# Two-byte count matrices, spread edge keys, early residual tiles, and seven block products in the last expert layer of a graph transformer kernel

## The chip, the cores and the metric

The kernel runs on one core of a Trainium2 chip. The metric is the device time of one execution in microseconds (us). Five engines work side by side and meet only at semaphores: PE (TensorE, matmuls and transposes), DVE (VectorE), ACT (ScalarE), POOL (GpSimd) and SP (SyncE), which here only issues transfers. All arithmetic on PE is fp32; the trace records each fp32 matmul as two MATMUL rows, so a row count is twice the number of matmuls in the code.

## What is computed

Two layers over a graph of 1250 nodes with 768 features. Each layer runs a linear-attention mixer, a two-step graph attention (GAT) and a mixture of experts, each with a residual. What matters here is cut from the reference:

```python
# edges: 10000 random pairs both ways + 1250 self loops (21250), sorted by dst
# layer 0 mixer: phi = exp(q @ rf.T - |q|^2/2); out = attn @ proj_w.T + proj_b
# layer 0 and 1 GAT, per head:
e     = leaky_relu(as_[src] + ad_[dst], 0.2)
m     = segment_max(e, dst);  w = exp(e - m[dst]);  z = segment_sum(w, dst)
out   = segment_sum(h[src] * (w / z[dst])[:, None], dst)
# layer 1 experts: 8 experts of width 128, top 2 of 8 per node
y     = sum_e gate[n, e] * (silu(x @ w1[e].T) @ w2[e].T)
```

The kernel doesn't walk edges in the GATs. It makes a dense 1250 x 1250 matrix that holds how often each (source, target) pair occurs, multiplies dense attention weights by it, and uses a second form of it (minus a large number where the count is zero) for the maxima.

## The kernel before

**Sizes.** Nodes are ten tiles of T = 125 rows (NT = 10). PSUM is split in two rings: five banks "V" drained by DVE and three banks "A" drained by ACT. `plan()` writes out by hand the order in which all banks are filled and drained; `V_AT` and `A_AT` give each its number, and `fill` on PE and `bank` on DVE and ACT follow it. A fill waits until the bank five (or three) fills back has been drained. All three engines run their queues strictly in order.

**Keys (the count of duplicates).** The 21250 edges lie as 125 x 170 (EC = 170 columns). `KEY` = source x 1250 + target. For each column, PE transposes the keys into a row (L550, four columns make one of 43 key groups) and DVE compares all pairs of that column (L1366), so that duplicates within one column are summed before they are scattered. After each fifth group DVE prepares 20 columns of indices (L1379 to L1383, `index_made`). `KEYS_BESIDE` and `KEYS_BESIDE_QK` say after which fill how many key groups stand: before, two behind each of the last 14 fills of the v product, and 15 groups among the six fills of the first q/k block. All 43 are done before the first head of the mixer.

**Scatter.** POOL issues 170 indirect DMAs (L2055), each adding 125 counts to `count_matrix0` or `count_matrix1` in DRAM (even and odd columns). Scatter c waits for the landing of scatter c - 2. The two matrices are fp32 and are first cleared by SP with two DMAs from `ZERO` (L2108 to L2110); POOL waits for `zeros_written`.

**Heads.** Eight heads of the mixer follow (`pk`, `pq` in ring A, `kv`, `num` in ring V; five more q/k blocks behind heads 0, 1, 3, 4 and 5), then the output is turned (L518), then the first half of the product h of GAT 0.

**Mask stage.** SP waits for the last landing of both matrices (L2201) and then loads them in ten blocks of 125 rows: `count_load(j)` loads block j of both. Buffers are three deep; load j waits until block j - 3 has been drained in its transposed form. `count_sum(j)` on DVE adds the two (L1503) and the self loop (L1505); PE's `mask(j)` turns the sum (L624), and DVE's `mask` writes the two-byte copy (L1513) and the NEG form (L1517) and calls `count_sum(j + 1)`. Between them PE makes the mixer's output product, two fills (`proj`, L507) for each node tile, and DVE's `project` adds them to the residual tile (L1489 for the bias, L1495 for the product). The residual tiles of x come through two slots (`SLOT_M`): SP loads tiles 0 and 1 behind the first three count blocks, and tile t + 2 when tile t has been stored (`residual`). Order on PE for t = 0 to 4: mask(2t), proj(t, 0), mask(2t + 1), proj(t, 1).

**Last expert layer.** Five chunks of 250 nodes. `up1(c)` makes the hidden rows of eight experts (ring A, 48 matmuls of 250 columns), ACT applies Silu (L1246), DVE multiplies by the gates (L1998). The down product of a chunk is four fills (two node tiles x two halves of 384 columns), each a sum over eight experts (L917): 32 matmuls. DVE adds each fill to the residual slot (L2011) and signals `slot_done`; SP stores the tile to `out` and then loads tile t + 2 to the same slot. On PE the order is up(2), down(1) and so on; down(3) is followed by down(4) with nothing between.

Of the kernel before, what the change touches and what calls it, by code (L numbers as in the profile page):

```python
# [31 lines left out]
KD = D // 128  # L32
# [23 lines left out]
KEYS_BESIDE = [0] * 6 + [2] * 14  # L56
KEYS_BESIDE_QK = [3, 3, 3, 2, 2, 2]
# [28 lines left out]

ASROW_AFTER = {4: (0, 1), 8: (2,)}
# [3 lines left out]
def plan():  # L91
# [50 lines left out]
    assert not keys  # L142
    for h in range(MH):
        A.extend(("pk", h, i) for i in range(5))
        A.extend(("pq", h, m, c) for m in range(2) for c in range(3))
        V.append(("kv", h))
        if h in BLOCK_AFTER:
            qk(BLOCK_AFTER[h])
        V.extend(("num", h, i) for i in range(2))
    turned("mix0")  # L150
# [44 lines left out]
    for c in range(6):  # L195
# [5 lines left out]
        if c > 0:  # L201
            V.extend(("g2", c - 1, i) for i in range(4))
# [3 lines left out]
def gps_kernel(nc, w, out):  # L206
# [6 lines left out]
    counts = [nc.dram_tensor(f"count_matrix{i}", [CNT, 1], F32).ap() for i in range(2)]  # L213
# [8 lines left out]
    with ctx:  # L222
# [111 lines left out]
        IDX_I = in_d(EC).bitcast(I32)  # L334
        TRASHI, TRASH = in_d(1).bitcast(I32), in_d(1)
# [4 lines left out]
        CS_OTHER = [mem(F_AT + 7108, N), mem(ROW_AT + N, N), mem(ROW_AT + 2 * N, N)]  # L340
# [82 lines left out]
        assert G_AT + 7480 <= K_AT  # L423
        LGT = mem(B_AT, N)
# [51 lines left out]
        gate_rows_loaded = [sem(f"gate_rows_loaded{i}") for i in range(4)]  # L476
        logits_turned = sem("logits_copied")
# [12 lines left out]
        def _(pe):  # L490
# [88 lines left out]
            for h in range(MH):  # L579
# [28 lines left out]
                for i in range(2):  # L608
# [6 lines left out]
                    last.then_inc(v_filled, 1)  # L615
            pe.wait_ge(v_drained, V_AT[("num", MH - 1, 1)] + 1)
# [248 lines left out]

            turn("lng", Y, lambda t: pe.wait_ge(tile_normed, 10 + t + 1), (0, 1))
# [24 lines left out]
            for c in range(6):  # L891
# [15 lines left out]
                if c > 0:  # L907
# [4 lines left out]
                    pe.wait_ge(gw2_loaded, 16)  # L912
                    for i in range(4):
# [348 lines left out]
        def _(dve):  # L1262
# [94 lines left out]
            def key_group():  # L1357
# [16 lines left out]
                if i % 5 == 4 or i == NKEY - 1:  # L1374
# [7 lines left out]
                    now(dve.tensor_tensor(s(IDXE), s(IDXE), s(KEY), ALU.add))  # L1382
                    dve.tensor_copy(s(IDX_I), s(IDXE)).then_inc(index_made, 1)  # L1383
# [73 lines left out]
            for h in range(MH):  # L1457
# [5 lines left out]
                for i in range(2):  # L1463
# [7 lines left out]
                                              r.unsqueeze(2).to_broadcast([T, 5, MD]), ALU.mult).then_inc(v_drained, 1)  # L1471
                if h < 3:
# [26 lines left out]
            def count_sum(j):  # L1499
# [3 lines left out]
                now(dve.tensor_tensor(c, c, CS_OTHER[j % 3][0:T], ALU.add))  # L1503
# [475 lines left out]

            for c in range(6):  # L1980
# [22 lines left out]
                if c > 0:  # L2003
                    for i in range(4):
# [16 lines left out]
        def _(pool):  # L2021
# [27 lines left out]
            for c in range(EC):  # L2049
# [3 lines left out]
                if c >= 2:  # L2053
                    pool.wait_ge(added[k], 16 * (c // 2))
                pool.indirect_dma_start(counts[k], bass.IndirectOffsetOnAxis(ap=IDX_I[0:T, c:c + 1].bitcast(U32), axis=0),  # L2055
                                        COUNT[0:T, c:c + 1], None, compute_op=ALU.add).then_inc(added[k], 16)
# [22 lines left out]
        def _(sp):  # L2079
# [119 lines left out]
            vf(("num", MH - 1, 1))  # L2199
            for k in range(2):  # L2200
                sp.wait_ge(added[k], 16 * (EC // 2))  # L2201

            def count_load(j):
                if j == 2:
                    af(("tr", "mix0", 2, KD - 1))
                if j >= 3:
                    vf(("mask", j - 3, 2))
                    sp.wait_ge(v_drained, V_AT[("mask", j - 3, 0)] + 1)
                for k, o in enumerate((CS[j % 3], CS_OTHER[j % 3])):
                    tile_load(o, counts[k][j * T * N:(j + 1) * T * N, :].rearrange("(p n) o -> p (n o)", p=T),  # L2210
                              count_loaded[j % 3])
# [183 lines left out]
```

## Time and profile before

| what | value |
|---|---|
| median of 3 runs | 2701.08 us (2700.16 to 2703.23) |
| the profiled execution: its time | 2700.95 us |
| the profiled execution: span of the trace | 2699.2 us |
| PE busy | 2602.6 us, 96% of the span |
| DVE, ACT, POOL busy | 56%, 29%, 13% |
| mean granted clock of PE | 0.988 of full |

The trace's times count from the start of the span; 1.75 us of the device time lie outside it. "Busy" on PE means that an instruction was in it, not that it ran at full clock. A bracket behind a row, such as [6.17 <-ACT arena L999], is the idle time of the engine just before it and what ended that idle time. DMA packets under 2 KB are many, since each scattered count is one of its own.

### The profile page before, as it was taken

Reading aid. Unit: us, or ns where it says so; the run is one execution under the profiler, and the core shown is the slowest. Engines: PE = TensorE matmul, PEld = TensorE weight load, DVE = VectorE, ACT = ScalarE, POOL = GpSimd, SP = SyncE. Lnnn points to the kernel's source line nnn. Section 1 sums busy time; section 2 is a strip of 40 time slices with the busy share of each in tenths; the row PEclk is TensorE's granted clock in tenths of the full one; section 3 lists DMA queues with packets and bytes.
Section 4 is the critical chain, followed back from the end, with each engine's and each line's share of the span. In section 5 each row is a group of like instructions: output and inputs, shape, how many; then the busy total and the mean of one; then the engine's idle time right before and its main releaser. Section 6 shows DMA issues by size and latency. Waiting matters only on the chain.

```text
span 2699.2 us, 26867 instructions
## 1 busy us (share of the span) xinstructions
PE 2602.6 (96%) x10759; PEld 1844.5 (68%) x10759; DVE 1519.7 (56%) x2596; ACT 780.1 (29%) x1314; POOL 346.8 (13%) x197
## 2 busy tenths in 40 slices
PE   7999999699999997999999999999999999999999
PEld 4667676457975987777777775555755786556776
DVE  4765451579948995997888997121332552341211
ACT  1044442006742773222222221420002331432000
POOL 0788888000000000000000000000000000000000
PEclk9999999899999998999999999999999999999999
DMA  9332322833020405000120004000250100212211
GB/s 313 56 42 22 43 11 28 226 111 129 19 59 0 105 10 209 1 1 1 70 99 0 23 23 162 18 1 35 71 166 18 35 1 1 69 71 80 85 35 46
DMA packets 138567, 168.40 MB, mean 62 GB/s; under 512 B 96509, under 2 KB 107607, under 8 KB 136915
## 3 DMA queue, kind: packets, MB, share of 16 engines
q1 hardware_dynamic: 67721, 166.21, 20.0%
q0 software_dynamic: 70720, 0.47, 2.7%
q8 instruction: 85, 1.39, 0.2%
q14 instruction: 41, 0.33, 0.0%
HBM read 124.00 MB, written 42.27 MB: 62 GB/s over the span
## 4 chain that ended last, share of the span: by engine, by line
PE 51%; DVE 7%; ACT 2%; issue 1%; DMA 0%; SPq 0%; DVEq 0%; ACTq 0%
PE psum L507 51%; DVE arena L1784 2%; DVE arena L1786 1%; DVE arena L1785 1%; DVE arena L1777 0%; ACT arena L1054 0%; ACT arena L1059 0%; ACT arena L945 0%; DVE arena L1444 0%; DVE arena L1850 0%; DVE arena L1288 0%; PE psum L518 0%; DVE arena L1783 0%; DVE arena L1776 0%; DVE arena L1809 0%
## 5 line engine op out<-in xcount | busy, mean ns | idle before, releaser
L507 PE MATMUL psum<-arena 128*125 128x384 f32 (+10 forms) x9848 | 2491.3, 414 | 41.4 <-DMA arena<-in_ffn_w 8.1
L507 PEld LDWEIGHTS psum<-arena 128*125 128x125 f32 (+3 forms) x9848 | 1740.6, 188 | 766.9 <-issue 138.7
L2055 POOL DMA_INDIRECT count_matrix<-arena x170 | 342.1, 2013 | 125.0 <-DVE arena L1383 63.6
L1784 DVE RECIPROCAL arena<-arena 128x500 f32<-128x500 f32 x60 | 196.7, 3278 | 2.1
L1534 DVE CUSTOM_DVE_ANT_0 arena<-arena 125x1250 bf16<-125x1250 bf16 (+1 forms) x100 | 139.2, 1456 | 12.6 <-ACT arena L1087 12.3
L1618 DVE TENSOR_TENSOR arena<-arena 125x1250 f32<-125x1250 f32 x80 | 116.3, 1453 | 18.9 <-ACT arena L1036 18.7
L2065 POOL MEMSET arena<- 125x60 f32 x1 | 0.2, 208 | 981.5 <-PE psum L507 981.5
L1033 ACT ACTIVATE arena<-arena 125x1250 f32<-125x1250 f32 x80 | 106.9, 1336 | 54.5 <-PE psum L507 54.2
L1621 DVE SCALAR_TENSOR_TENSOR arena<-arena 125x1250 f32<-125x1250 f32 x80 | 116.9, 1461 | 2.8
L988 ACT ACTIVATE arena<-arena 32x500 f32<-32x500 f32 (+1 forms) x108 | 59.1, 548 | 177.4 <-DVE arena L1417 176.6
L945 ACT ACTIVATE arena<-psum 128x250 f32<-128x250 f32 (+1 forms) x102 | 40.8, 491 | 238.9 <-PE psum L518 238.4
L1179 ACT ACTIVATE arena<-psum,arena 128x250 f32<-128x250 f32 x120 | 49.3, 465 | 200.6 <-PE psum L507 200.6
L1036 ACT ACTIVATE arena<-arena 125x1250 f32<-125x1250 f32 x80 | 105.8, 1322 | 0.0
L518 PE MATMUL psum<-arena 125*128 125x125 f32 x420 | 58.3, 284 | 23.8 <-DVE arena L1307 10.8
L1078 ACT ACTIVATE arena<-psum 125x384 f32<-125x384 f32 x80 | 38.6, 487 | 139.7 <-PE psum L507 139.7
L1171 ACT ACTIVATE arena<-arena 128x500 f32<-128x500 f32 x60 | 37.2, 621 | 140.0 <-DVE arena L1768 139.9
L1054 ACT ACTIVATE arena<-arena 125x250 f32<-125x250 f32 x100 | 40.4, 490 | 116.4 <-PE psum L507 116.4
L518 PEld LDWEIGHTS psum<-arena 125*128 125x128 f32 x420 | 46.0, 144 | 37.2 <-issue 18.8
L1640 DVE TENSOR_TENSOR arena<-arena 125x2500 f32<-125x2500 f32 x10 | 27.6, 2763 | 72.9 <-ACT arena L1059 72.9
L1552 DVE TENSOR_SCALAR arena<-arena 125x40 f32<-125x40 f32 (+1 forms) x4 | 0.7, 178 | 106.5 <-ACT arena L1078 78.3
L2011 DVE TENSOR_TENSOR arena<-psum,arena 125x384 f32<-125x384 f32 x20 | 11.1, 557 | 87.4 <-PE psum L507 87.4
L1768 DVE TENSOR_SCALAR arena<-arena 128x500 f32<-128x500 f32 x60 | 25.0, 420 | 62.7 <-ACT arena L1179 61.3
(204 smaller groups left out, 1407.2 us busy)
## 6 DMA issues: line engine op xcount, KB each, us to landing
arena<-in_ffn_w SPq DMA_DIRECT2D x3, 4608.0 KB, 14.0
count_matrix<-arena SPq DMA_DIRECT2D x2, 6250.0 KB, 38.8
arena<-count_matrix SPq DMA_DIRECT2D x20, 546.9 KB
residual<-arena SPq DMA_DIRECT2D x30, 336.0 KB
arena<-residual SPq DMA_DIRECT2D x30, 336.0 KB
arena<-target_rows SPq DMA_DIRECT2D x12, 610.4 KB
arena<-in_gat_w SPq DMA_DIRECT2D x3, 2304.0 KB, 17.0
arena<-residual SPq DMA_DIRECT2D x10, 672.0 KB
```

The costliest lines, as they stand in the source:

```text
L507: return pe.matmul(o, lhsT, rhs, start=start, stop=stop, skip_group_check=share)
L518: last = pe.transpose(b[:, i * T:(i + 1) * T], source[0:T, t0 + i, k * 128:(k + 1) * 128], IDENT[0:T, 0:T])
L945: act.activation(o, i, ACT.Copy).then_inc(a_drained, 1)
L988: act.activation(o[low, cols], t[32 * i:32 * i + 32, cols], ACT.Square)
L1033: act.activation(ET4[n % 4][0:T, :], PROWS[layer][h % 2][0][0:T, :], ACT.Exp, bias=ASC[0:T, h, j:j + 1])
L1036: act.activation(E24[n % 2][0:T, :], PROWS[layer][h % 2][1][0:T, :], ACT.Exp, bias=AS2[0:T, h, j:j + 1]).then_inc(slopes_made, 1)
L1179: last = act.activation(HB[u % 2][:, m, :], b[:, j * 250:(j + 1) * 250], ACT.Identity, bias=B1C[:, e, m:m + 1])
L1534: ins = dve.tensor_tensor_reduce(SUMS[n % 2][0:T] if layer < 2 else E24[n % 2][0:T, :], NEG[0:T, t, :], ASROWS[layer][h % 2][0:T, :], 1.0, ...
L1618: dve.tensor_tensor(et, et, E24[n % 2][0:T], ALU.max).then_inc(larger_made, 1)
L1621: dve.scalar_tensor_tensor(et, et, 1.0, CT[0:T, j, :], ALU.min, ALU.mult).then_inc(et_made, 1)
L1784: now(dve.reciprocal(t_, t_))
L2055: pool.indirect_dma_start(counts[k], bass.IndirectOffsetOnAxis(ap=IDX_I[0:T, c:c + 1].bitcast(U32), axis=0), COUNT[0:T, c:c + 1], None, co ...
```

## The change

Four edits come together.

1. The count matrices in DRAM hold 16-bit integers. The clearing, the scattered additions (from a 16-bit copy of COUNT, one more DVE cast for each batch of indices) and the block loads move half the bytes; `count_sum` adds two 16-bit operands into the same fp32 tile.
2. The 43 key groups are placed otherwise: 17 beside the v product (the first five behind its tiles 6 and 7), one behind each of the six fills of the first q/k block, and four behind each of the heads 0 to 4.
3. Residual tiles 0 and 1 of x are loaded before SP waits for the scatter; later count loads wait only for `count_summed` of the block three back, and each group of them stands behind the residual load of its step (`COUNTS_BESIDE`).
4. In the last expert layer the down products of chunks 1 to 4 use seven block products of four matmuls in place of eight (Winograd's form). DVE makes four sums of the hidden blocks for each chunk (`gated_sums`) and four sums of weight blocks once. Some products are shared by several outputs: PE fills a bank, DVE adds it to one slot, PE goes on accumulating in the same bank, DVE adds it to another. Two semaphores, `parts_filled` and `parts_read`, order that.

```diff
-KEYS_BESIDE = [0] * 6 + [2] * 14
-KEYS_BESIDE_QK = [3, 3, 3, 2, 2, 2]
+KEYS_BESIDE = [0] * 6 + [2, 3] + [1] * 12
+KEYS_BESIDE_QK = [1] * 6
+KEYS_AFTER_HEAD = [4] * 5 + [0] * 3
+COUNTS_BESIDE = {0: (3,), 1: (4,), 2: (5, 6), 3: (7, 8), 4: (9,)}
...
-    counts = [nc.dram_tensor(f"count_matrix{i}", [CNT, 1], F32).ap() for i in range(2)]
+    counts = [nc.dram_tensor(f"count_matrix{i}", [CNT, 1], U16).ap() for i in range(2)]
...
+                for _ in range(KEYS_AFTER_HEAD[h]):      # on PE, behind the fills of head h
+                    key_rows()
...
+            def down1(c):
+                low, high = slice(0, 4), slice(4, 8)
+                tile = [slice(0, T), slice(T, 2 * T)]
+                ga, gs = GA[c % 2], GS[c % 2]
+                left = [ga[:, low, tile[0]], ga[:, high, tile[0]], gs[:, 3], ga[:, high, tile[1]], gs[:, 0], gs[:, 1], gs[:, 2]]
+                right = [GW2[:, low, 0:HALF], GW2[:, high, 0:HALF], GW2[:, high, HALF:], GT[:, 2], GT[:, 0], GT[:, 1],
+                         GW2[:, low, HALF:]]
+                bank_b, bank_c, bank_a = (fill("V", ("g2", c, i)) for i in "bca")
+                n = 4 * (c - 1)
+                def product(i, b, done, begin=False):
+                    for e in range(4):
+                        last = mm(b[0:T, 0:HALF], left[i - 1][:, e, :], right[i - 1][:, e, :], begin and e == 0, e == 3,
+                                  share=True)
+                    last.then_inc(done, 1)
+                product(1, bank_a, parts_filled, True)
+                pe.wait_ge(ga_sums, c)
+                pe.wait_ge(gw2_sums, 1)
+                product(5, bank_b, parts_filled, True)
+                pe.wait_ge(parts_read, n + 1)
+                product(6, bank_a, parts_filled)
+                pe.wait_ge(parts_read, n + 2)
+                product(3, bank_b, v_filled)
+                pe.wait_ge(parts_read, n + 3)
+                product(7, bank_a, parts_filled)
+                product(2, bank_c, v_filled, True)
+                pe.wait_ge(parts_read, n + 4)
+                product(4, bank_a, v_filled)
...
+                    step(dve.tensor_copy(s(COUNT_I), s(COUNT)))
+                    after(own[0])
                     dve.tensor_copy(s(IDX_I), s(IDXE)).then_inc(index_made, 1)
...
-                now(dve.tensor_tensor(c, c, CS_OTHER[j % 3][0:T], ALU.add))
+                now(dve.tensor_tensor(c, COUNTS[j % 3][0:T, 0], COUNTS[j % 3][0:T, 1], ALU.add))
...
+            def gated_sums(c):
+                a, s = GA[c % 2], GS[c % 2]
+                a11, a12, a21, a22 = (a[:, 4 * j:4 * j + 4, i * T:(i + 1) * T] for i in range(2) for j in range(2))
+                step(dve.tensor_tensor(s[:, 2], a11, a21, ALU.subtract))
+                now(dve.tensor_tensor(s[:, 0], a21, a22, ALU.add))
+                now(dve.tensor_tensor(s[:, 1], s[:, 0], a11, ALU.subtract))
+                dve.tensor_tensor(s[:, 3], a12, s[:, 1], ALU.subtract).then_inc(ga_sums, 1)
+            def drain_parts(c):
...
+                dve.wait_ge(parts_filled, n + 1)
+                add(bank_a, 0, 0, parts_read)
+                s[1] = slot(SLOT_2)
+                dve.wait_ge(parts_filled, n + 2)
+                add(bank_b, 1, 1, parts_read)
+                dve.wait_ge(parts_filled, n + 3)
+                add(bank_a, 0, 1, parts_read)
+                dve.wait_ge(v_filled, V_AT[("g2", c, "b")] + 1)
...
+                add(bank_b, 0, 1, v_drained)
+                dve.wait_ge(parts_filled, n + 4)
+                add(bank_a, 1, 1, parts_read)
+                dve.wait_ge(v_filled, V_AT[("g2", c, "c")] + 1)
+                add(bank_c, 0, 0, v_drained)
+                dve.wait_ge(v_drained, count[0] - 1)
+                finished()
+                dve.wait_ge(v_filled, V_AT[("g2", c, "a")] + 1)
+                add(bank_a, 1, 0, v_drained)
...
+                    gated_sums(c)
+                if c > 1:
+                    drain_parts(c - 1)
+                if c == 1:
+                    dve.wait_ge(gw2_loaded, 16)
...
+                    now(dve.tensor_tensor(GT[:, 0], w12, w11, ALU.subtract))
+                    now(dve.tensor_tensor(GT[:, 1], w22, GT[:, 0], ALU.subtract))
+                    now(dve.tensor_tensor(GT[:, 2], w21, GT[:, 1], ALU.subtract))
...
+                    dve.tensor_tensor(w12, w22, w12, ALU.subtract).then_inc(gw2_sums, 1)
...
-                load(counts[k].rearrange("(p c n) o -> p c (n o)", p=128, c=NT),
-                     ZERO.unsqueeze(1).to_broadcast([128, NT, N]), zeros_written)
+                load(counts[k].rearrange("(p c n) o -> p c (n o)", p=128, c=NT // 2),
+                     ZERO.bitcast(U16).unsqueeze(1).to_broadcast([128, NT // 2, 2 * N]), zeros_written)
...
             vf(("num", MH - 1, 1))
+            for t in range(2):
+                residual_get(0, x, SLOT_M, t)
             for k in range(2):
                 sp.wait_ge(added[k], 16 * (EC // 2))
             def count_load(j):
-                if j == 2:
-                    af(("tr", "mix0", 2, KD - 1))
                 if j >= 3:
-                    vf(("mask", j - 3, 2))
-                    sp.wait_ge(v_drained, V_AT[("mask", j - 3, 0)] + 1)
+                    sp.wait_ge(count_summed, j - 2)
...
-            residual(0, x, SLOT_M, res[XMID0],
-                     beside=lambda t: count_load((3, 4, 6, 8)[t]) if t < 4 else None,
-                     behind=lambda t: count_load((5, 7, 9)[t]) if t < 3 else None)
+            residual(0, x, SLOT_M, res[XMID0], later_counts, begun=True)
```

## Rows read from the trace of the kernel before

**Rows 1.** The page: busy time of the engines, share of the span, instructions.
```profile
PE 2602.6 (96%) x10759; PEld 1844.5 (68%) x10759; DVE 1519.7 (56%) x2596; ACT 780.1 (29%) x1314; POOL 346.8 (13%) x197
```
**Rows 2.** Who waited for whom, PE: total us, times, longest.
```profile
PE psum L624 <- DVE arena L1505: 23.8, 6, 9.1
...
PE psum L507 <- ACT arena L999: 6.2, 1, 6.2
```
**Rows 3.** PE in order of time, mask stage: start, us, what, idle before.
```profile
482.15 2.43 PE L624 MATMUL psum<-arena 125*125 125x125 f32 x10 [9.10 <-DVE arena L1505]
...
497.50 2.46 PE L624 MATMUL psum<-arena 125*125 125x125 f32 x10 [8.55 <-DVE arena L1505]
499.76 5.41 PE L507 MATMUL psum<-arena 128*125 128x384 f32 x12
...
510.85 1.35 PE L624 MATMUL psum<-arena 125*125 125x125 f32 x10 [0.71 <-DVE arena L1505]
...
515.91 1.25 PE L624 MATMUL psum<-arena 125*125 125x125 f32 x10
517.00 4.04 PE L507 MATMUL psum<-arena 128*125 128x384 f32 x12
...
553.64 2.60 PE L633 MATMUL psum<-arena 125*128 125x125 f32 x20
```
**Rows 4.** DVE in order of time, same stage.
```profile
480.11 1.46 DVE L1503 TENSOR_TENSOR arena<-arena 125x1250 f32<-125x1250 f32 x1 [55.24 <-DMA arena<-count_matrix]
...
492.45 0.96 DVE L1489 TENSOR_TENSOR arena<-arena 125x768 f32<-125x768 f32 x1 [10.46 <-DMA arena<-in_x]
493.45 0.81 DVE L1513 CAST arena<-arena 125x1250 uint16<-125x1250 f32 x1
```
**Rows 5.** SP's queue in order of time, same stage.
```profile
472.36 5.95 SPq L2081 DMA_DIRECT2D arena<-count_matrix  x12
478.35 1.62 SPq L2081 DMA_DIRECT2D arena<-in_x  x4
```
**Rows 6.** POOL in order of time, the scatter.
```profile
67.13 2.13 POOL L2055 DMA_INDIRECT count_matrix<-arena  x1 [63.57 <-DVE arena L1383]
...
77.69 1.99 POOL L2055 DMA_INDIRECT count_matrix<-arena  x1 [3.19 <-DMA count_matrix<-arena]
...
468.68 1.99 POOL L2055 DMA_INDIRECT count_matrix<-arena  x1 [0.30 <-issue]
```
**Rows 7.** POOL: who waited for whom, over the span.
```profile
POOL count_matrix L2055 <- DMA count_matrix<-arena: 14.7, 17, 3.2
```
**Rows 8.** The tile count_matrix: landing of the two clearing DMAs.
```profile
L2081 SPq DMA_DIRECT2D count_matrix<-arena x2: 8340/8716/9091, 11.6 to 20.0; - x2
...
DMA to landing us min/median/max: 34.4/38.8/43.1
```
**Rows 9.** DVE in order of time, first batch of keys.
```profile
56.83 0.34 DVE L1366 SCALAR_TENSOR_TENSOR arena<-psum,arena 125x125 f32<-125x125 f32 x1
...
65.98 0.18 DVE L1383 CAST arena<-arena 125x20 int32<-125x20 f32 x1
```
**Rows 10.** Two stretches: length, busy PE PEld DVE ACT POOL, clock, DMA share, GB/s.
```profile
150.00:200.00 50.00, 43.83 (x181) 28.91 (x181) 26.00 (x64) 22.09 (x41) 43.52 (x22) 0.93 0.28 24
...
482.20:497.50 15.30, 6.75 (x22) 4.53 (x22) 4.98 (x8) 0.00 (x0) 0.00 (x0) 0.72 0.74 179
```
**Rows 11.** Last expert layer: PE, DVE and SP in order of time.
```profile
2528.94 166.41 PE L507 MATMUL psum<-arena 128*125 128x384 f32 x608 [0.84 <-DVE arena L1992]
...
2572.96 0.68 DVE L1998 TENSOR_TENSOR arena<-arena 128x500 f32<-128x500 f32 x1 [4.38 <-ACT arena L1246]
...
2665.07 0.77 SPq L2081 DMA_DIRECT2D out<-arena  x2
2668.01 0.76 SPq L2081 DMA_DIRECT2D arena<-residual  x2
...
2695.38 0.56 DVE L2011 TENSOR_TENSOR arena<-psum,arena 125x384 f32<-125x384 f32 x1 [4.60 <-PE psum L507]
```

More of the change, by code:

```diff
@@ L141, in plan @@
     qk(0)
-    assert not keys
     for h in range(MH):
@@ L149, in plan @@
         V.extend(("num", h, i) for i in range(2))
+        some_keys(KEYS_AFTER_HEAD[h])
+    assert not keys
     turned("mix0")
@@ L201, in plan @@
         if c > 0:
-            V.extend(("g2", c - 1, i) for i in range(4))
+            V.extend(("g2", c - 1, i) for i in (range(4) if c == 1 else "bca"))
     return V, A
@@ L334, in gps_kernel @@
         IDX_I = in_d(EC).bitcast(I32)
+        COUNT_I = in_d((EC + 1) // 2).bitcast(U16)[:, 0:EC]
         TRASHI, TRASH = in_d(1).bitcast(I32), in_d(1)
@@ L423, in gps_kernel @@
         assert G_AT + 7480 <= K_AT
+        GT = mem(G_AT + 7488, 3, 4, HALF)
+        assert G_AT + 7488 + 3 * 4 * HALF <= K_AT
+        GS = [mem(C_AT + 2000 + i * 2000, 4, 4, T) for i in range(2)]
         LGT = mem(B_AT, N)
@@ L1471, in _ @@
                                               r.unsqueeze(2).to_broadcast([T, 5, MD]), ALU.mult).then_inc(v_drained, 1)
+                for _ in range(KEYS_AFTER_HEAD[h]):
+                    key_group()
                 if h < 3:
@@ L1978, in _, with add, finished @@
             dve.tensor_tensor(GG[0:T], GG[0:T], wide(RMX), ALU.mult).then_inc(gates_made, 1)
+            def gated_sums(c):
[6 more added lines that the diff above has]
+            def drain_parts(c):
+                n = 4 * (c - 1)
+                s = [slot(SLOT_2), None]
+                half = [slice(0, HALF), slice(HALF, D)]
+                bank_b, bank_c, bank_a = (bank(("g2", c, i)) for i in "bca")
+                def add(b, tt, h, done):
+                    o = s[tt][:, half[h]]
+                    dve.tensor_tensor(o, b[0:T, 0:HALF], o, ALU.add).then_inc(done, 1)
+                def finished():
+                    dve.engine_nop().then_inc(slot_done, 1)
+                dve.wait_ge(parts_filled, n + 1)
[6 more added lines that the diff above has]
+                dve.wait_ge(v_filled, V_AT[("g2", c, "b")] + 1)
+                dve.wait_ge(parts_read, n + 3)
+                add(bank_b, 0, 1, v_drained)
[7 more added lines that the diff above has]
+                add(bank_a, 1, 0, v_drained)
+                dve.wait_ge(v_drained, count[0])
+                dve.wait_ge(parts_read, n + 4)
+                finished()
             for c in range(6):
@@ L2203, in count_load @@
             def count_load(j):
-                if j == 2:
-                    af(("tr", "mix0", 2, KD - 1))
                 if j >= 3:
-                    vf(("mask", j - 3, 2))
-                    sp.wait_ge(v_drained, V_AT[("mask", j - 3, 0)] + 1)
-                for k, o in enumerate((CS[j % 3], CS_OTHER[j % 3])):
-                    tile_load(o, counts[k][j * T * N:(j + 1) * T * N, :].rearrange("(p n) o -> p (n o)", p=T),
+                    sp.wait_ge(count_summed, j - 2)
+                for k in range(2):
+                    tile_load(COUNTS[j % 3][:, k, :], counts[k][j * T * N:(j + 1) * T * N, :].rearrange("(p n) o -> p (n o)", p=T),
                               count_loaded[j % 3])
```

16 lines of the change are left out of this document (13 added, 3 removed).

## The prediction

> **What bounds the kernel now.** I read the page first. PE is busy for 96% of the span [rows 1], so a gain must come from PE's idle time, from time at the lower of its two clocks (1.2 in place of 2.4 GHz), or from fewer matmuls. The view of who waited for whom names the largest idle entry: the mask transposes (L624) stood still for 23.8 us in six waits, behind DVE's count sums (L1505); behind ACT's first exponentials (L999) PE lost 6.2 us [rows 2].
>
> PE's order of time places the six waits: 9.10 us before mask(0), 8.55 us before mask(1), 6.15 us over four later ones, of which 0.71 is the shortest. The stage runs from 482.15 to 553.64, 71.5 us [rows 3]. One mask and one fill, without a wait, take 1.09 + 4.04 = 5.13 us, ten of them 51.3. With 14.7 us of waits inside the stage, 5.4 us are left: work at the lower clock. Transposes took 2.46 us in place of 1.25, a fill 5.41 in place of 4.04 [rows 3], and the granted clock from 482 to 497 us was 0.72 [rows 10].
>
> Who is late? DVE's first count sum waited for the count load [rows 4], SP issued that load at 472.36 [rows 5], behind the last scatter, which POOL ended at 468.68 + 1.99 = 470.67 [rows 6]; it landed 1.7 us later. DVE's second sum stood behind the bias addition of residual tile 0, which sat idle for 10.46 us for that tile [rows 4], issued at 478.35 behind twelve count DMAs [rows 5]. PE was ready for mask(0) at 482.15 - 9.10 = 473.05. So mask(0) is set by the chain first batch of keys, 170 scatters, count load, sum; mask(1) by the residual tile.
>
> **The start of the scatter.** POOL starts at 67.13, 1.0 after the cast of the first index batch ended (65.98 + 0.18) [rows 6, 9]. Now the fifth key group follows tile 7. DVE's compares of that tile begin at 56.83 [rows 9]; a group takes about 1.2 us (four compares at some 0.27 between starts, and a semaphore), three take 3.6, the preparation 0.95, the new cast 0.2: 61.5, and POOL at 62.5. That is 4.6 earlier. It needs cleared matrices by then. They now land at 46.0 and 63.1 [rows 8]; at half the bytes both have landed when the first one lands now, about 46, so they don't bind.
>
> **The pace of the scatter.** 17 issues waited 14.7 us for landings [rows 7], 9.6 more than the 0.30 us that every issue has. Some 4 us of this fall into the first 30 us, the longest 3.19 [rows 6], while the start-up loads still run. 6.25 MB fewer in front of these end them some 16 us earlier. I take 3.5 off; the bounds are 0 and 9.6. The other scatters I leave at their 2.3 us: each landed about 1.7 after its issue ended, and the one two back may take about 2.6 before POOL feels it. A two-byte addition appears in no row; the four-byte one is the nearest.
>
> **The later key batches** must not starve POOL. A batch of 20 lasts 46 us. From 62 on, batches are wanted at 108, 154, 200, 247, 293, 339, 385 and 431. Five groups behind five tiles of about 4.5 us, then six in the q/k block, give the first three in time (about 85, 105 and 130). Heads run from 157 to 425; eight at 17 us and five q/k blocks of 26 us make their ends 200, 243, 260, 303 and 346, and the batches behind them (247 to 431) are all ready before they are wanted. PE makes the same 170 transposes. DVE has some 13 us from a head's last fill to the next kv fill, and 4.8 (keys) + 4.5 (score weights) in it. Were this cover gone, 6 us of slack before mask(0), worked out next, would hide it.
>
> **The head of the kernel** gets shorter on PE, and this is worth nothing. With 9 fewer groups in the q/k block and 11 fewer before it, DVE keeps up with the block; the wait of 6.17 shrinks to about 1.5 (ACT's table load and last squares), and the 3.5 us of clock (0.93 over 50 us [rows 10]) return. PE comes to mask(0) at about 473.05 - 8.2 = 464.9, but the counts come later.
>
> **The count load.** From issue to the sum 480.11 - 472.36 = 7.75 us [rows 4, 5]. The first pair has half the bytes. Bounds: 7.75, and 4.4 (four issues at about 0.4 and a store of a residual tile, 2.94 from issue to the next load [rows 11]). I take 5.1, nearer the second since it has the smaller size: 2.65 off. So mask(0) starts at 482.15 - 4.6 - 3.5 - 2.65 = 471.4, which is **10.75 us** earlier, with a wait of 6.5.
>
> **The mask stage.** Residual tiles 0 and 1 land in the scatter's last 40 us, so the wait of 8.55 goes: project(0) adds its bias while mask(0) is turned, and DVE then needs 1.58 for NEG and 1.75 for the sum against PE's fill of 4.04. In the steady state a tile's load is issued 3 us after the tile two before is done, and wanted 10 us after; the waits of up to 2.7 us shrink to the 0.71 of DVE's own chain (bias, cast, NEG and sum against one fill), four times, 2.8. Of the lower clock I leave a third, 1.7, since one idle stretch in front remains. 51.3 + 2.8 + 1.7 = 55.8: **15.7 us** off. Bounds: 20 (no wait inside, no lower clock) and 10 (only the 8.55 and its clock go).
>
> Here a rule can be weighed against the row. The sum is held at the 1.46 of its row [rows 4]; the nearest row with a two-byte operand is the cast of the same width, 0.81. At 0.81 the 0.71 waits go too, 2.8 us more. By the Trainium skill, page VectorE: DVE Perf Modes, section What auto-detection actually checks, two-input work gets the faster mode only if every tensor is 16-bit; here the output is fp32, so the rule says 1.46. No row before shows the mixed form.
>
> **The last layer.** A fill of eight matmuls takes 4.60 + 0.56 = 5.16 us [rows 11], 0.645 each; 4 chunks x 4 fewer make 10.3 us off. What it adds lies on DVE. Let G be the time at which PE begins down(c - 1). The last gated product ended at 2572.96 + 0.68, 1.35 after ACT's bank was filled [rows 11]; four sums at 0.7 end at G + 4.15, the first addition at G + 4.7. PE needs it behind two products, at G + 5.16: 0.45 to spare. All later additions lie under a product of 2.58. The weight sums (four of 1536 elements; by the rows of 768 and 1250 elements [rows 4] about 1.8 each, an estimate) lie under down(0), whose four fills fit the ring of five. Only down(4) has no up product in front. Tile 6 is done at G - 1.95, its store takes 2.94 to the next load [rows 11], the load the same: G + 3.9, in time. Tile 7 is done at G + 0.6, SP comes to it at G + 1.7, its slot is full at G + 7.6 and its addition ends at G + 8.15 where PE wants it at G + 7.74: 0.4 lost. The tail behind the last addition (2695.94 to 2699.2) stays, 0.1 more for two stores close together. **9.8 us** off; bounds 10.3 and, with 1.5 us lost in each chunk, 4.
>
> **Sum.** 10.75 + 15.7 + 9.8 = 36.25. All between 553 and 2529 us moves with it: the maxima on DVE begin with proj(5), the saved masks behind the last residual tile. The profiled execution took 2700.95 (span 2699.2 and 1.75 around it): 2664.7. The median of the runs is 0.13 above that: 2664.8.
>
> **Rivals.** (a) The mask stage stays bound by DMA: residual tiles and count loads collide at the new places, the four later waits stay, and the stage gives 10 in place of 15.7: 2670 to 2674. For it: in this stretch DMA ran at 0.74 busy [rows 10]; against: half the count bytes. (b) Last layer: the two-way handshake takes back most of the saving, 1.5 us in each chunk, since 0.45 us is a thin margin: 2671. (c) By the rows of the lower clock, micro-waits at every product would do worse: 5.41 against 4.04 [rows 3] on chunks of 18.1 us costs 6 us each, 24 in all, the layer then loses 14: 2688. The Trainium skill, page TensorE: Matmul & The Clock Gate, section A second HAM failure mode: psum-queue depth-cycling, tells of such swinging of the clock; this trace shows none between the fills of the last layer. (d) Slower: the landing of a two-byte addition. If it takes longer than 2.6 us, each scatter waits for the one two back. 36 us are used up at 0.22 us more for each of 169 scatters, a landing of about 2.8 in place of 1.7; at 3.7 the kernel is some 75 us slower. Against it: nothing but size changes in the descriptors. (e) More than forecast: all waits in the mask stage go and POOL loses no landing wait: 2655.
>
> **Chances.** Forecast 0.57 (own range 2660 to 2669); (a) 0.13, (b) 0.10, (c) 0.03, (d) 0.05, (e) 0.09; that two parts give nothing and the third little, no change, 0.03. Less than 0.2% (5.4 us) can't be told from nothing by a measurement of this kernel. Faster 0.92, same 0.03, slower 0.05. Range 2656 to 2682: it takes in (a) and (b) together and most of (e).
>
> **What would show it.** POOL's first scatter near 62.5, its last near 460; mask(0) on PE near 471 after 6 us of idle time; no wait above 1 us before the other masks; 576 matmul rows in place of 608 in the last layer with no idle time above 0.5. The scatter's pace is the step that I trust least: if POOL's rows show landing waits all along, (d) holds. If PE waits for DVE's additions (L2011's successors), (b).

## The result, and the profile after

The changed kernel takes 2668.99 us (median of 4 runs, 2667.01 to 2671.09) against 2700.62 before: a ratio of 0.9882, 95% interval 0.9869 to 0.9896, 31.6 us or 1.2% less. The forecast was 2664.8 with a range of 2656 to 2682, faster. The profiled execution of the changed kernel took 2667.01 us with a span of 2665.3, 33.9 less than the span before. One of the four executions of e7 below took 3040.3 us at a mean granted clock of 0.849, and e7's median below is that of the other three.

Four landmarks on PE cut the span: the start of mask(0), the end of the mask stage (the first rows of column transposes, L633 before and L645 after), the first down product of the last layer, and the end.

| us | before | changed | difference | forecast |
|---|---|---|---|---|
| start of mask(0) | 482.15 | 474.64 | -7.5 | -10.75 |
| mask stage | 71.49 | 53.82 | -17.7 | -15.7 |
| from there to the first down product | 1975.30 | 1974.57 | -0.7 | 0 |
| first down product to the end of the span | 170.26 | 162.27 | -8.0 | -9.8 |
| sum | 2699.2 | 2665.3 | -33.9 | -36.25 |

The first view is PE in order of time in the mask stage of the changed kernel, the answer to [rows 3]:

```profile
434.22 39.77 PE L517 MATMUL psum<-arena 128*125 128x392 f32 x120 [0.47 <-ACT arena L991]
474.64 1.35 PE L636 MATMUL psum<-arena 125*125 125x125 f32 x10 [0.65 <-ACT arena L1124]
475.83 4.04 PE L517 MATMUL psum<-arena 128*125 128x384 f32 x12
479.76 1.35 PE L636 MATMUL psum<-arena 125*125 125x125 f32 x10
...
490.67 1.35 PE L636 MATMUL psum<-arena 125*125 125x125 f32 x10 [0.71 <-DVE arena L1555]
...
528.46 2.60 PE L645 MATMUL psum<-arena 125*128 125x125 f32 x20
```

The 8.55 us before mask(1) are gone and the 9.10 before mask(0) are 0.65; the four later waits are 0.71 or 0.72 each, and every transpose group takes 1.25 or 1.35, every fill 4.04: no work at the lower clock. But the wait before mask(0) is not the forecast 6.5 us for the count sum. It is 0.65, and it names ACT (the last copy of h, which PE must see before it starts the stage). PE came at 434.22 + 39.77 = 473.99, 0.9 later than before, where the prediction had it 8.2 earlier. The 0.9 is within the spread: the six profiled executions below with these key places came between 473.99 and 475.21, the three with the old places between 473.05 and 475.62.

DVE, SP and POOL in order of time (the answers to [rows 4], [rows 5] and [rows 6]) show how the counts fared:

```profile
472.15 1.46 DVE L1553 TENSOR_TENSOR arena<-arena 125x1250 f32<-125x1250 uint16 x1 [46.35 <-DMA arena<-count_matrix]
473.65 0.29 DVE L1555 TENSOR_TENSOR arena<-arena 125x125 f32<-125x125 f32 x1
```

```profile
426.04 1.60 SPq L2187 DMA_DIRECT2D arena<-in_x  x4
467.08 14.23 SPq L2187 DMA_DIRECT2D arena<-count_matrix  x20
```

```profile
62.97 2.13 POOL L2161 DMA_INDIRECT count_matrix<-arena  x1 [59.41 <-DVE arena L1431]
...
463.31 1.99 POOL L2161 DMA_INDIRECT count_matrix<-arena  x1 [0.30 <-issue]
```

The scatter starts at 62.97 (forecast 62.5), its last issue is at 463.31 (before 468.68), SP issues the first count load at 467.08 and DVE sums it at 472.15: 5.07 us, forecast 5.1. The sum is complete at 473.94. Two chains, PE's own work and the scatter, meet at mask(0) within 0.1 us. PE starts some 0.25 us after the end of a sum that it waited for (before: 481.61 + 0.29 on DVE, 482.15 on PE), so the counts would have let it start at 474.2; PE's own work and ACT's copy let it start at 474.64.

The head of the kernel, PE and then DVE in order of time:

```profile
145.44 41.68 PE L517 MATMUL psum<-arena 128*125 128x256 f32 x172 [2.85 <-ACT arena L1045]
186.95 1.50 PE L560 MATMUL psum<-arena 125*125 125x125 f32 x12
189.77 0.67 PE L560 MATMUL psum<-arena 125*125 125x125 f32 x4 [1.32 <-DVE arena L1518]
...
298.44 1.93 PE L560 MATMUL psum<-arena 125*125 125x125 f32 x16
```

```profile
188.10 0.42 DVE L1456 TENSOR_TENSOR arena<-arena 32x250 f32<-32x250 f32 x1
188.54 0.16 DVE L1516 TENSOR_SCALAR arena<-psum 125x5 f32<-125x5 f32 x1
188.74 0.19 DVE L1517 RECIPROCAL arena<-arena 125x5 f32<-125x5 f32 x1
188.97 0.66 DVE L1518 TENSOR_TENSOR arena<-psum,arena 125x480 f32<-125x480 f32 x1
...
298.36 0.16 DVE L1516 TENSOR_SCALAR arena<-psum 125x5 f32<-125x5 f32 x1
```

ACT's wait at the first head fell from 6.17 to 2.85 us. Behind head 0 PE transposes three key groups and then stands for 1.32 us at the fourth. The fourth group wants the bank five fills back, the head's first num fill, and DVE comes to it only at 188.54, behind the folds of the q/k block (the additions of the squares, L1454 to L1456). The same wait stands behind heads 1 and 4; together 4.0 us. Head 2 has no q/k block and no wait. Head 3 has both a block and a fourth group and yet no wait: the folds of its block have two additions in place of three, so DVE is at the num fill at 298.36, before PE's first transposes (298.44), and not 1.6 us behind them as at head 0.

The last layer on PE, on DVE and in SP's queue (the answer to [rows 11]):

```profile
2503.03 142.97 PE L517 MATMUL psum<-arena 128*125 128x384 f32 x536 [0.94 <-DVE arena L2087]
2646.20 2.85 PE L517 MATMUL psum<-arena 128*125 128x384 f32 x8 [0.20 <-DVE arena L2048]
2650.52 10.59 PE L517 MATMUL psum<-arena 128*125 128x384 f32 x32 [1.48 <-DVE arena L2048]
```

```profile
2550.16 0.55 DVE L2048 TENSOR_TENSOR arena<-psum,arena 125x384 f32<-125x384 f32 x1
2551.45 0.56 DVE L2048 TENSOR_TENSOR arena<-psum,arena 125x384 f32<-125x384 f32 x1 [0.73 <-PE psum L517]
...
2645.59 0.56 DVE L2048 TENSOR_TENSOR arena<-psum,arena 125x384 f32<-125x384 f32 x1 [4.15 <-DMA arena<-residual]
2649.91 1.02 DVE L2048 TENSOR_TENSOR arena<-psum,arena 125x384 f32<-125x384 f32 x2 [3.76 <-DMA arena<-residual]
```

```profile
2638.94 2.02 SPq L2187 DMA_DIRECT2D out<-arena  x2
2642.38 0.76 SPq L2187 DMA_DIRECT2D arena<-residual  x2
2643.18 0.79 SPq L2187 DMA_DIRECT2D out<-arena  x2
2646.65 0.76 SPq L2187 DMA_DIRECT2D arena<-residual  x2
```

In chunk 1 DVE's first addition is at 2550.16 and DVE then idles 0.73 us for the second product: the handshake fits, no wait on PE. In the last chunk DVE waits for the residual tiles. Tile 7's store is issued at 2643.18, tile 9's load at 2646.65, and its addition starts at 2649.91; PE loses 0.20 and 1.48 us.

### The profile page after: what moved, and what is told of

Same layout as the page of the kernel before. It is cut to its first block, busy times and chain, and to the rows that moved or that the text cites. A ratio compares the mean times of both kernels' runs of the same rounds, so it can differ in the third digit from the quotient of the medians.

```text
span 2665.3 us, 26854 instructions
## 1 busy us (share of the span) xinstructions
PE 2586.9 (97%) x10727; PEld 1835.0 (69%) x10727; DVE 1546.5 (58%) x2637; ACT 780.0 (29%) x1314; POOL 347.5 (13%) x197
## 4 chain that ended last, share of the span: by engine, by line
PE 51%; DVE 7%; ACT 2%; DMA 1%; issue 1%; SPq 0%; DVEq 0%; ACTq 0%
PE psum L517 51%; DVE arena L1834 2%; DVE arena L1836 1%; DVE arena L1835 1%; DVE arena L1827 0%; ACT arena L1100 0%; ACT arena L1105 0%; ACT arena L991 0%; DVE arena L1492 0%; DVE arena L1900 0%; PE psum L528 0%; DVE arena L1334 0%; DVE arena L1833 0%; DVE arena L1826 0%; DVE arena L1859 0%
## 5 line engine op out<-in xcount | busy, mean ns | idle before, releaser
L1690 DVE TENSOR_TENSOR arena<-arena 125x2500 f32<-125x2500 f32 x10 | 27.6, 2763 | 72.8 <-ACT arena L1105 72.8
L1463 DVE TENSOR_SCALAR arena<-psum,arena 96x500 f32<-96x500 f32 (+1 forms) x36 | 23.3, 647 | 66.0 <-PE psum L517 65.6
```

## The experiments

The table takes the same landmarks from each profiled execution. "Arrival" is the start of mask(0) less the wait in front of it; "two-byte" says what the count matrices hold. Each median is compared with runs of the kernel before, made beside it (2700.6 to 2700.8).

| run | scatter first to last issue | PE arrival | mask(0) | mask stage | last layer | median | ratio to before (95%) |
|---|---|---|---|---|---|---|---|
| before | 67.1 to 468.7 | 473.05 | 482.15 | 71.5 | 170.3 | 2700.6 | |
| changed | 63.0 to 463.3 | 473.99 | 474.64 | 53.8 | 162.3 | 2669.0 | 0.9882 (0.9869, 0.9896) |
| e1 last layer only | 68.8 to 472.7 | 475.62 | 486.30 | 70.0 | 159.9 | 2691.7 | 0.9967 (0.9952, 0.9981) |
| e2 old key places | 68.0 to 468.2 | 474.42 | 478.50 | 55.3 | 162.6 | 2674.1 | 0.9908 (0.9890, 0.9926) |
| e3 four-byte counts | 63.5 to 466.8 | 474.62 | 479.35 | 65.2 | 162.6 | 2683.2 | 0.9941 (0.9922, 0.9961) |
| e4 late residual tiles | 63.6 to 464.7 | 474.50 | 475.58 | 60.7 | 162.2 | 2673.7 | 0.9900 (0.9883, 0.9916) |
| e5 8 scatters left out | 63.9 to 446.7 | 474.84 | 475.49 | 53.8 | 162.3 | 2668.4 | 0.9883 (0.9867, 0.9900) |
| e6 three keys a head | 63.4 to 464.2 | 468.26 | 475.07 | 56.1 | 159.9 | 2670.9 | 0.9894 (0.9878, 0.9911) |
| e7 e5 and e6 | 63.4 to 442.2 | 468.21 | 468.86 | 53.8 | 161.7 | 2660.5 | 0.9857 (0.9838, 0.9877) |
| e8 extra slots | 64.0 to 465.3 | 475.21 | 475.86 | 53.8 | 160.1 | 2668.5 | 0.9888 (0.9871, 0.9904) |
| e9 early keys, slots | 54.0 to 455.8 | 470.66 | 471.31 | 53.8 | 158.0 | 2658.9 | 0.9848 (0.9834, 0.9861) |
| e10 changed again | 63.5 to 466.8 | 474.51 | 477.47 | 56.6 | 160.5 | 2670.0 | 0.9888 (0.9873, 0.9903) |

From the mask stage's end to the first down product all of them took 1973.8 to 1976.2 us. So no edit reaches in there beyond this spread: what the stage gives is neither lost nor added to before the last layer.

One execution of each kernel was profiled, and the same code doesn't give the same landmarks each time. Before and e1 have the same code up to the last layer, and mask(0) differs by 4.2 us; changed and e10 are one kernel, and it differs by 2.8. So a landmark says which wait stands there, and the medians say better what an edit is worth.

### e1: the last layer's edit alone

The kernel before with `down1`, `gated_sums`, `drain_parts`, the weight sums and their plan; nothing else.

```diff
 # the kernel before, with
-            V.extend(("g2", c - 1, i) for i in range(4))
+            V.extend(("g2", c - 1, i) for i in (range(4) if c == 1 else "bca"))
...
+                    if c > 1:
+                        down1(c - 1)
+                        continue
```

> The kernel before with the last expert layer's edit alone. Theory: the edit is worth what the last layer shows in the changed kernel (162.3 us in place of 170.3 from the first down product to the end), 8.0 us, whatever stands in front: 2692.6, with two waits of PE for the residual slots, 0.2 and 1.5 us, before products 6 and 3 of the last chunk. Rival: the waits come from some shift of DMA traffic by the other edits; alone it gives the 9.8 us forecast, 2690.8, and no wait above 0.5.

Measured 2691.73 us, 9.0 below the runs beside it. Its last layer took 159.9 us, 10.3 less than before, with one wait of 1.66 on PE (two were expected). The difference to the changed kernel's 162.3 isn't the edit. Two stretches of the same work, the first 10 us of it, changed kernel first, e1 second (columns as in [rows 10]):

```profile
2503.00:2513.00 10.00, 9.97 (x25) 5.71 (x26) 6.52 (x9) 0.00 (x0) 0.00 (x0) 0.80 0.95 394
```

```profile
2530.00:2540.00 10.00, 9.93 (x31) 5.88 (x32) 7.41 (x11) 0.00 (x0) 0.00 (x0) 1.00 0.91 378
```

At a granted clock of 0.80, 25 matmul rows started in 10 us, at 1.00 it was 31. That is worth 2 us, and it falls one way or the other from execution to execution: e6 and e10, with the changed kernel's code there, had 1.00 as well and took 159.9 and 160.5. (That e3 stands at 162.6 with 1.00 is chance: its waits for slots were longer, 2.6 us, and its last 32 rows took 12.28 in place of 10.59.) The execution profiled before was at 0.78 in its first 10 us, so against it the edit is worth the changed kernel's 8.0. The slot wait is there without the other edits, so the rival in the expectation (a shift of other traffic) is out.

### e2: the old places of the keys

```diff
-KEYS_BESIDE = [0] * 6 + [2, 3] + [1] * 12
-KEYS_BESIDE_QK = [1] * 6
-KEYS_AFTER_HEAD = [4] * 5 + [0] * 3
+KEYS_BESIDE = [0] * 6 + [2] * 14
+KEYS_BESIDE_QK = [3, 3, 3, 2, 2, 2]
+KEYS_AFTER_HEAD = [0] * 8
```

> The changed kernel with the old places of the 43 key groups. Theory: spreading the keys moved PE's arrival at the mask stage by almost nothing (3.3 us won at the first head, 4.0 lost in three waits behind heads 0, 1 and 4), but it starts the scatter 4.2 us earlier; undone, the first scatter is at 67 and mask(0) starts 3 to 4 us later than 474.6, with PE waiting for the count sum: 2672 to 2673 beside 2669 for the changed kernel. Rival (the placement is worth nothing, since PE is the later one at mask(0)): mask(0) stays within 1 us of 474.6.

Measured 2674.12, 5.1 above the changed kernel; mask(0) at 478.50, 3.9 later, behind a wait of 4.08 for the count sum:

```profile
478.50 1.34 PE L636 MATMUL psum<-arena 125*125 125x125 f32 x10 [4.08 <-DVE arena L1555]
```

PE arrives at 474.42, against 473.99 and 474.51 in the two executions of the changed kernel. The new key places gave PE nothing; they gave the scatter 4 to 5 us at its start (67.99, against 62.97 to 64.03 in the executions with the new ones). The profile alone wouldn't rule out the rival, since mask(0) came at 477.47 in e10; the times do: the lowest of e2's four, 2673.5, is above all eight of the changed kernel and e10 (2667.0 to 2671.1).

### e3: four-byte counts

```diff
-    counts = [nc.dram_tensor(f"count_matrix{i}", [CNT, 1], U16).ap() for i in range(2)]
+    counts = [nc.dram_tensor(f"count_matrix{i}", [CNT, 1], F32).ap() for i in range(2)]
...
-                if j >= 3:
-                    sp.wait_ge(count_summed, j - 2)
+                if j == 2:
+                    af(("tr", "mix0", 2, KD - 1))
+                if j >= 3:
+                    vf(("mask", j - 3, 2))
+                    sp.wait_ge(v_drained, V_AT[("mask", j - 3, 0)] + 1)
```

> The changed kernel with four-byte count matrices and, since the buffers then hold the sums too, the old waits of the count loads; early residual tiles, key places and last layer stay. Theory (bytes matter in three places): both matrices are cleared at about 63, the first scatter follows at 64 (1 us later), early landings cost 2 us, the first count load takes 7.7 in place of 5.1: mask(0) near 480; later masks wait 1 to 6 us in all, and some low clock returns: 2676 to 2681. Rival (bytes don't matter, the early residual tiles alone repaired the stage): 2669 to 2671.

Measured 2683.22, 14 above the changed kernel and more than expected. PE's masks:

```profile
479.35 2.43 PE L635 MATMUL psum<-arena 125*125 125x125 f32 x10 [4.73 <-DVE arena L1552]
497.35 1.35 PE L635 MATMUL psum<-arena 125*125 125x125 f32 x10 [0.71 <-DVE arena L1552]
509.91 1.40 PE L635 MATMUL psum<-arena 125*125 125x125 f32 x10 [2.37 <-DVE arena L1552]
525.75 2.46 PE L635 MATMUL psum<-arena 125*125 125x125 f32 x10 [3.96 <-DVE arena L1552]
```

The first count load shows the bytes best: the last scatter was issued at 466.77, in e10 at 466.82, and from SP's issue to the sum it took 6.86 us, where the two-byte kernels took 4.54 to 5.19; mask(0) is 1.9 later than in e10. Mask(1) doesn't wait, since the residual tiles are early. Later masks wait 2.37 and 3.96 us, and two groups run at half speed (2.43, 2.46). So the early tiles alone repair the 8.55 us and not the rest; the stage takes 65.2 us, and 11.4 of the 17.7 won hang on the bytes together with the later waits of the count loads, which this kernel could not separate. 2.1 of the 11.4 are slow work behind the wait of 4.73 before mask(0); e10 has such work too, in a stage of 56.6. The two clearing DMAs landed 34.4 and 43.3 us after their issue, and the scatter started at 63.5 behind them, the same place as in e10 (two-byte, landing after 27.2 and 27.6): at the scatter's start the bytes bought next to nothing. For e9, whose scatter starts at 54.0, a clearing that lands at 63.2 would have come too late; that is reckoned, not run. The scatter's length from first to last issue is 403.3 here, 401.6 and 403.9 in before and e1, and 400.3 to 403.3 over seven two-byte kernels, mean 401.3 against 402.9. Some 1.6 us may be won in landings; the spread is as large.

### e4: residual tiles 0 and 1 behind the counts

```diff
-            for t in range(2):
-                residual_get(0, x, SLOT_M, t)
...
-            residual(0, x, SLOT_M, res[XMID0], later_counts, begun=True)
+            residual(0, x, SLOT_M, res[XMID0], later_counts)
```

> The changed kernel with residual tiles 0 and 1 loaded behind the first three count blocks, as before. Theory: mask(0) stays at 474.6; tile 0 is issued at 471.6 and lands near 480, so that mask(1) waits about 5 us where it waited 8.6 in the kernel before, plus 1 to 2 us of low clock: 2674 to 2676. Rival (with half the count bytes in front the tile comes in time): within 1 us of 2669.

Measured 2673.74, 4.7 above; the lowest of the four, 2672.4, is above all of the changed kernel's. PE before mask(1), and DVE's bias addition in front of it:

```profile
484.99 2.46 PE L636 MATMUL psum<-arena 125*125 125x125 f32 x10 [4.21 <-DVE arena L1555]
```

```profile
479.94 0.96 DVE L1539 TENSOR_TENSOR arena<-arena 125x768 f32<-125x768 f32 x1 [4.52 <-DMA arena<-in_x]
```

The wait returns at 4.21 us, where the two executions of the old stage had 8.55 and 6.05, with 2.6 us of low clock in the stage (60.7 against 53.8, 4.2 of it the wait). All later waits stay at 0.71 or 0.72. Both are needed: the place of the tiles for mask(1), and the bytes, or the later waits of the count loads that go with them in e3, for the masks behind it.

### e5, e6 and e7: which chain holds mask(0)?

e5 leaves out the last 8 of 170 scatters (these edges are missing in the counts). e6 puts three key groups behind each of six heads. e7 does both.

```diff
 # e5, e7
-            for c in range(EC):
+            for c in range(EC - 8):
...
 # e6, e7
-KEYS_BESIDE = [0] * 6 + [2, 3] + [1] * 12
+KEYS_BESIDE = [0] * 6 + [2, 3] + [1] * 10 + [2, 2]
-KEYS_AFTER_HEAD = [4] * 5 + [0] * 3
+KEYS_AFTER_HEAD = [3] * 6 + [0] * 2
```

> The changed kernel with the last 8 of the 170 scatters left out (these edges are missing in the counts), which ends the scatter 18 us earlier. Theory (in the changed kernel PE's arrival at 474.0 and the count sum at 473.9 are level): mask(0) doesn't move, 474.6, and the time stays within 1 us of 2669. Rival (the scatter still sets mask(0), as forecast): mask(0) up to 3 us earlier.

> The changed kernel with three key groups behind each of the heads 0 to 5 (and two more beside the v product) in place of four behind heads 0 to 4. Theory (the fourth group needs the bank of the head's first num fill, which DVE drains late): the three waits of 1.32 us vanish, PE comes to mask(0) at about 470 in place of 474.0 and then waits 4 us for the count sum; mask(0) at about 474, time within 1 us of 2669. Rival (PE alone binds): mask(0) at 470.5, 2665. Rival 2 (the waits belong to any transposes behind a head): the waits stay.

> Both: the last 8 scatters left out and three key groups behind each head. Theory (two chains level at mask(0); only both shortened together move it): mask(0) near 470.6, 4 us earlier, 2665. Rival (something else, as ACT's last copies of h, holds mask(0)): stays at 474.6.

PE at mask(0) in e6, then in e7:

```profile
475.07 2.43 PE L636 MATMUL psum<-arena 125*125 125x125 f32 x10 [6.81 <-DVE arena L1555]
```

```profile
468.86 1.35 PE L636 MATMUL psum<-arena 125*125 125x125 f32 x10 [0.65 <-ACT arena L1124]
```

A scatter that ends 17 us earlier doesn't move mask(0) (e5: 475.49, 2668.4). A PE that arrives 5.7 us earlier doesn't either (e6: 475.07, 2670.9); it waits 6.81 us, and the low clock after that wait makes the stage 2.2 us longer. Both together move it by 5.8 and give 2660.5, 8.5 below the changed kernel (6.5 between the profiled executions). In e6 no wait for L1518 is left behind the heads: it belongs to the fourth group, as the theory had it. I expected PE at 470; it came at 468.3. Of the 1.8 more, 1.5 is the block behind ACT's wait, 40.19 us in e6 against the 41.68 shown above for the same 172 rows: in its first 3 us the granted clock was 1.00, in the changed kernel 0.50. This is hardly chance, as it is in the last layer: e6 and e7 share their key places and both took 40.19, and the seven others with a block of 172 rows 41.60 to 41.88. How the key places bring it about is open.

### e8: two more residual slots in the last layer

Tiles 8 and 9 get slots of their own, loaded when tile 6 is done.

```diff
+        SLOT_E = [mem(C_AT + 6000 + i * D, D) for i in range(2)]
...
+                    if extra and t >= 6:
+                        if t == 6:
+                            for i in (8, 9):
+                                residual_get(n_pass, src, extra, i)
+                        continue
```

> The changed kernel with two further residual slots for tiles 8 and 9, loaded as soon as tile 6 is done, without waiting for the stores of tiles 6 and 7. Theory (the waits of 0.2 and 1.5 us in the last chunk are the slots' round trip): both vanish, the last layer takes 160.6 us in place of 162.3, 2667.3. Rival (DVE's additions or the handshake are late anyway): waits stay.

The last layer is one stretch without a wait:

```profile
2504.93 155.92 PE L518 MATMUL psum<-arena 128*125 128x384 f32 x576 [0.94 <-DVE arena L2089]
```

160.1 us to the end against 162.3: the waits were the slots' round trip. The granted clock in the first 10 us was 0.79 here and 0.80 there, so the two can be compared. The median, 2668.48, is within the runs' spread of 2669; the gain of 2 us is seen in the trace and not in the times.

### e9 and e10: all findings together, and the changed kernel once more

```diff
-KEYS_BESIDE = [0] * 6 + [2, 3] + [1] * 12
+KEYS_BESIDE = [0] * 4 + [2, 3] + [1] * 14
-KEYS_AFTER_HEAD = [4] * 5 + [0] * 3
+KEYS_AFTER_HEAD = [3] * 6 + [0] * 2
 # and the slots of e8
```

> The changed kernel with its first five key groups behind tiles 4 and 5 of the v product (in place of 6 and 7), one behind each later fill, three behind each of the heads 0 to 5, and the two extra residual slots. Theory (two chains meet at mask(0), both must be shortened; then the last layer's slot waits): the first scatter starts near 53 in place of 63, the count sum is ready near 464, PE comes at 468.3, mask(0) at 469, 6 us earlier and with no low clock; the last layer loses no wait: 7.5 to 8 us less than the changed kernel, about 2661. Rival (an earlier scatter collides with the start-up loads and the clearing, as its first landings did in the kernel before): the scatter ends no earlier than 460, mask(0) near 471 and 2664.

> The changed kernel once more, unaltered, on the same chip as the run before it, for the comparison: 2669, its first down product near 2503 and the end 162 us later, or 160 if the clock of PE is full in the first 10 us of it.

e9 takes 2658.88 us, 41.9 less than before (1.5%) and 11.1 less than the changed kernel beside it. POOL's start and DVE's count sum in e9:

```profile
54.01 2.14 POOL L2163 DMA_INDIRECT count_matrix<-arena  x1 [50.44 <-DVE arena L1432]
```

```profile
464.17 1.46 DVE L1554 TENSOR_TENSOR arena<-arena 125x1250 f32<-125x1250 uint16 x1 [41.70 <-DMA arena<-count_matrix]
```

The counts are ready at 465.95, PE comes at 470.66 and goes on at 471.31 without a dip of the clock. Now PE's own work is the bound. It came 2.4 us later than in e6: 1.6 in the block of 172 rows (41.78), 0.8 before it. The rival, an earlier scatter that ends no sooner than 460, falls: the last issue is at 455.75. The last layer of e9 and e10 can be compared, since both had a clock of 1.00 in its first 10 us: 158.0 against 160.5, so the slots are worth 2.5 there.

e10 shows how even the two chains of the changed kernel are: the same code, but its scatter ended 3.5 us later than in the first profile, so that PE waited 2.96 us for the sum and a transpose group ran at half speed:

```profile
477.47 2.43 PE L636 MATMUL psum<-arena 125*125 125x125 f32 x10 [2.96 <-DVE arena L1555]
```

## Why the prediction was right, and where it was off

**Direction and size.** Faster as said, 31.6 us where 36 were forecast. The chain that was named (keys, scatter, count load, sum, with the residual tile behind it) is the one that the experiments confirm: e2, e3 and e4 each undo one link and lose 5, 14 and 5 us. The 2668.99 us lie at the edge of the forecast's own range (2660 to 2669), and what was off had both signs: 3.2 and 1.8 us too much was forecast for mask(0) and the last layer, 2.0 too little for the mask stage. (The profiled execution is also the fastest of the four, 2.0 below their median, so the 33.9 us between the profiles flatter the change a little.)

**The start of the scatter**: 62.97 against 62.5. Right in size. That the cleared matrices don't bind holds (issued at 11.5 and 19.7, landed 25.8 to 26.9 later, so by 46.6 at the latest). e3 shows that they hardly bound at four bytes either.

**The pace of the scatter**: the term of 3.5 us was too large. POOL's waits for landings, the answer to [rows 7]:

```profile
POOL count_matrix L2161 <- DMA count_matrix<-arena: 12.5, 17, 1.6
```

Two us less than before, 14.9 in e10, no less at all. Rival (d), a slower landing of two-byte additions, is out: it would make every scatter wait, and in the nine two-byte kernels 13 to 20 waited, 2.9 us at the most. The later key batches didn't starve POOL either, as forecast: in the changed kernel it waited for DVE's indices once, at the start.

**The count load** 5.07 against 5.1, **the sum's duration** 1.46 against 1.46. The rule that the prediction weighed (the Trainium skill, page VectorE: DVE Perf Modes, section What auto-detection actually checks) agrees with the trace: L1553 with 16-bit inputs and an fp32 output takes 1.46 us, as with fp32 inputs.

**The head of the kernel** is the step that failed in its mechanism. "PE comes to mask(0) at about 473.05 - 8.2 = 464.9" was wrong by 9 us. Three parts: ACT's wait fell to 2.85, not 1.5 (1.35); the sentence that DVE has some 13 us behind a head looked only forward, to the next kv fill, and left out that a key fill itself needs a bank which DVE drains behind the folds: 4.0 us; and the clock's 3.5 us didn't come back. The first 3 us behind ACT's wait ran at 0.50 as before, and the same 428 rows took 97.5 us where they had taken 97.65. The 3.5 were also too large: in e6, with 1.00 from the start, the rows took 96.0. The 0.93 of [rows 10] covers the wait of 6.17 itself, in which a low clock costs nothing. e2 measures the sum of it all as zero. The 6 us of slack were to have hidden such a mishap, and they were used up by it. With the forecast's own slack at 6.5 and an error of 9, mask(0) came at PE's arrival in place of the counts'. That this cost only half a microsecond is luck: the counts were 2.8 late themselves. Had they come as forecast, PE alone would have held mask(0) at 474.64.

**mask(0)** therefore at 474.64 in place of 471.4: 0.5 from POOL's start, 2.3 from the pace (400.3 us from first to last issue, where 401.6 - 3.5 was forecast), 0.4 from PE and ACT.

**The mask stage**: the one wait of 8.55 gone, the four of 0.71 left, as forecast, 53.8 against 55.8. The 1.7 us left for low clock weren't needed, as PE didn't stand for 6.5 us in front; in e6, where it did stand 6.8, they were (2.2). Rival (a) fell: no two-byte kernel shows a wait above 0.72 us behind mask(1).

**The last layer**: 8.0 against 9.8. The sixteen matmuls fewer gave the 10.3 forecast within 0.1: e8, without slot waits and at nearly the clock of before in the first 10 us (0.79, before 0.78), took 160.1, which is 10.2 less. The handshake cost nothing, with 0.73 us of DVE idle time where 0.45 was reckoned, so rival (b) fell too. The slot round trip was mis-sized: 0.4 forecast, 1.7 measured (store to load 3.47 in place of 2.94, the load 3.3 in place of 2.9, and the store of tile 6 took 2.02 us to issue in place of 0.77). The rest, 0.6, lies in bubbles at the waits and in a tail 0.3 longer. Rival (c), a swinging clock from the handshake: between 2550 and 2640 the granted clock is 1.00, so it isn't seen here.

What stays open: how e3's 11 us divide between bytes and waits of the count loads, how the key places of e6 and e7 keep the clock up at the first head, and what puts the clock at 0.80 or 1.00 in the first 10 us of the last layer.

## What to carry to other kernels

When a long stall is cut, write down the arrival of every chain at that point, with its own error. Here two chains ended within half a microsecond of each other, and each experiment on one alone moved nothing (e5, e6); in e6 the slow work behind the longer wait took back 2.2 us besides. Both together gave 8.5 us. And a fill that is inserted in a ring of banks has a price backward too: ask who drained the bank it takes, and behind what.

## What the runs showed of the hardware

A scatter of 125 two-byte additions costs POOL the same 1.99 us as one of four-byte additions and lands about as soon: POOL waited 9.3 to 15.1 us in all for landings in the two-byte kernels, 14.7 before and 15.8 in e1. An idle stretch of PE can cost more than itself: 6.8 us of waiting brought 2.2 us of slow work behind it (e6), 4.2 us 2.6 (e4), 4.1 us 1.5 (e2) and 3.0 us 2.8 (e10). So the price doesn't grow with the wait. The waits of 0.71 in the mask stage, and one of 2.05 in the kernel before, brought none. The same code ran its first 10 us in the last layer at a granted clock of 0.80 or of 1.00, 2 us apart, from one execution to another; a difference of that size between two single profiles of this kernel says nothing of an edit.
